# The FFN's input blocks turned by VectorE instead of TensorE in an attention-FFN kernel

## The chip, the cores and the metric

The kernel runs on one core of a Trainium2 chip. The metric is the device time of one execution in microseconds. The core has five engines that run their own instruction streams and wait for one another on semaphores: TensorE (PE; PEld is its weight load), VectorE (DVE), ScalarE (ACT), GpSimd (POOL) and SyncE (SP), whose work here is to issue transfers. Sixteen DMA engines carry the transfers of all queues.

## The reference

Four sequences of 2048 tokens of width 512, in float32. One attention layer, then a feed-forward layer (FFN), each followed by a LayerNorm:

```python
x = layernorm(x + attention(x) + x)          # causal, one head of width 512, its own LayerNorm with gamma, beta inside
probs = softmax(x @ wr.T)                    # router, 8 experts
routes, indices = top_k(probs, 2)
gates = routes / routes.sum(-1)
h = silu(x @ w1.T); h = silu(h @ w3.T); h = h @ w2.T
out = zeros_like(x)
for k in range(2): out = out.at[indices[:, k]].add(gates[:, k] * h)
x = layernorm(x + out)
```

Since `indices` are below 8, only the first eight rows of `out` get anything: sums over all 8192 tokens, weighted with their gates. The kernel therefore adds up the gated second hidden layer for each expert and multiplies the eight sums by `w2` at the very end. All other output rows are a LayerNorm of the attention's output.

## The kernel before

A float32 product is made of three passes with rounded operands (`split_product`, L330 to L335): high x high, high x low, low x high, on tiles of 128x128 weights and 128x512 data. Each operand is split by ScalarE, which writes the rounded high part, and VectorE, which subtracts it to get the low part.

**Attention** runs over four batches of 16 tiles of 128 query rows. It stores its normalised output x1 to a scratch tensor in DRAM, tile by tile, through SP's queue. In the last batch's tiles `load_w13` and `split_w13` bring in and split the FFN weights, which take the places of attention's weights (`m_hi` and `wvo_hi` in the rows stand for w1 and w3).

**The FFN** runs over 16 groups (`group(i, ...)` on each engine) of 512 tokens, one block of x1 of 512x512 each. A block is loaded to one half of `x1_in` with tokens on the partitions, two groups ahead (L401 to L405 on SP; the first two blocks by ScalarE's queue in its tile 14 of the last batch, L688 to L695). For the products it must have the features on the partitions. TensorE turns it in 16 transposes of 128x128 by the identity into PSUM banks 0 to 3 (`turn_x1`, L1279 to L1282); ScalarE rounds each bank to `x1t_hi` (L729 to L731), VectorE subtracts (`split_x1`, L1018 to L1020). For the next group's block eight transposes stand between the first and the second product, eight behind the second product's third tile, since they need banks that the products have left. The first block's 16 stand behind the last attention tile.

A group on TensorE: eight router matmuls (L1297 to L1299), the first product of 48 matmuls (with the last gate of the group before and four transposes of the router's logits behind its first quarter), eight transposes, the second product of 48 with two of the four gates (`gate`, L1284 to L1291) and eight transposes in it, and a third gate behind. The gates need the router's result. That comes by a chain: the logits are turned, VectorE subtracts the row maximum (`shifted`, L1039), POOL makes the exponential as a power (`expo`, L513), VectorE finds the two best and makes the gates (L1043 to L1069). In between VectorE subtracts for the first product's four Silu outputs (`split_h1`, L1026 to L1028) as ScalarE delivers them: the second and third behind `shifted`, the fourth behind the arg-max (L1054). The second product's chunk c waits for the c-th of them:

```python
for c in range(DC):
    if n == 0:
        pe.wait_ge(h1_ready, i * 4 + c + 1)
```

Each engine works through its instructions in the order in which they are written; nothing reorders them. Loops over batches and groups are hardware loops, with the last turn written out.

## Time and profile before

| | |
|---|---|
| time, median of 3 runs | 1711.9 us (1708.99 to 1712.27) |
| profiled execution, its own time | 1712.2 us |
| its span, first to last instruction | 1710.4 us |
| granted TensorE clock, mean | 0.997 |
| busy: PE, DVE, ACT, POOL | 98%, 46%, 39%, 17% of the span |
| FFN groups | the last 460 us of the span |

Rows of a timeline give the start in us from the span's start, the duration in us, the engine, the line of the kernel, the operation with what it writes and reads, and how often it stands in a row. In brackets is the time for which the engine was idle before, and what released it. A matmul's row runs to its modelled end, so rows of TensorE overlap; the distance of two starts tells what a step takes. The names are the program's without numbers: `x_in` is `x1_in`, `h_lo` is `h1_lo` or `h2_lo`.

### The profile page before, as it was taken

To read this page: it belongs to the slowest core of one execution; us is meant where nothing else is said; L and a number is where in the kernel's file an instruction comes from. 1 tells how busy PE (TensorE), PEld (TensorE's weight loads), DVE (VectorE), ACT (ScalarE), POOL (GpSimd) and SP (SyncE) were. 2 spreads that over 40 slices of the span, in tenths; PEclk is the share of its full clock that TensorE was granted. 3 is DMA by queue.
4 is the path that set the end of the run, shared out by engine and by line. 5 is a ranking of instruction groups with operands and counts; after the bars stand their busy time and mean duration, and the time that the engine had idled before them with its cause. 6 is when DMAs were issued, how large, how long until landed. Compare 5 with 4: busy or idle time off the path is not lost.

```text
span 1710.4 us, 23965 instructions
## 1 busy us (share of the span) xinstructions
PE 1680.0 (98%) x8179; PEld 1399.9 (82%) x8179; DVE 788.9 (46%) x2104; ACT 670.6 (39%) x1301; POOL 283.8 (17%) x491
## 2 busy tenths in 40 slices
PE   7999999999999999999999999999999999999998
PEld 5888888878888887888888888888878888888886
DVE  5454443455353455445334554534444444444443
ACT  4443433343342344344234443423344444444442
POOL 1120101121120111112011212201122121212111
PEclk9999999999999999999999999999999999999999
DMA  4111101121120112121111221112220101010100
GB/s 154 56 55 45 68 31 38 62 85 59 56 68 31 38 58 74 62 69 61 38 38 49 71 70 70 50 39 71 80 107 33 49 25 49 25 49 25 49 0 7
DMA packets 50116, 92.58 MB, mean 54 GB/s; under 512 B 5456, under 2 KB 5456, under 8 KB 50016
## 3 DMA queue, kind: packets, MB, share of 16 engines
q1 hardware_dynamic: 38064, 70.31, 11.7%
q10 hardware_dynamic: 11952, 20.99, 3.9%
q8 instruction: 57, 0.93, 0.2%
q14 instruction: 43, 0.35, 0.1%
HBM read 57.71 MB, written 33.57 MB: 53 GB/s over the span
## 4 chain that ended last, share of the span: by engine, by line
PE 80%; issue 12%; POOL 3%; ACT 3%; DVE 1%; DMA 0%; ACTq 0%; POOLq 0%; DVEq 0%
PE psum L333 24%; PE psum L335 24%; PE psum L334 23%; PE psum L1189 3%; PE psum L1281 2%; PE psum L1127 1%; POOL rstd L438 1%; ACT xin L564 1%; PE psum L1299 1%; PE psum L1298 1%; PE psum L1291 1%; PE psum L1290 1%; POOL expo L513 1%; ACT affine L548 1%; ACT tok L564 1%
## 5 line engine op out<-in xcount | busy, mean ns | idle before, releaser
L333 PE MATMUL psum<-xt_hi,g_hi 128*128 128x512 f32 (+3 forms) x640 | 240.2, 375 | 0.4 <-DVE g_lo L837 0.4
L335 PE MATMUL psum<-xt_lo,g_hi 128*128 128x512 f32 (+3 forms) x640 | 230.4, 360 | 0.0
L612 ACT ACTIVATE pt_hi<-psum 128x512 fp32r<-128x512 f32 (+3 forms) x160 | 84.9, 531 | 369.2 <-PE psum L1189 363.4
L334 PE MATMUL psum<-xt_hi,g_lo 128*128 128x512 f32 (+3 forms) x640 | 229.6, 359 | 0.0
L333 PE MATMUL psum<-v_hi,pt_hi 128*128 128x512 f32 x544 | 222.9, 410 | 1.6 <-DVE pt_lo L847 1.1
L335 PE MATMUL psum<-v_lo,pt_hi 128*128 128x512 f32 x544 | 213.1, 392 | 0.0
L334 PE MATMUL psum<-v_hi,pt_lo 128*128 128x512 f32 x544 | 212.8, 391 | 0.0
L435 POOL TENSOR_TENSOR var_eps<-meanvar,eps 128x2 f32<-128x2 f32 (+1 forms) x97 | 19.4, 200 | 1055.9 <-DVE meanvar L815 1051.5
L852 DVE TENSOR_REDUCE rowmax<-psum 128x1 f32<-128x512 f32 (+3 forms) x160 | 97.6, 610 | 198.3 <-PE psum L335 197.6
L734 ACT ACTIVATE act_f<-psum 128x512 f32<-128x512 f32 x128 | 76.6, 598 | 235.2 <-PE psum L335 235.2
L513 POOL TENSOR_TENSOR expo<-euler,shifted 128x32 f32<-128x32 f32 x16 | 87.3, 5457 | 319.5 <-DVE shifted L1039 319.5
L333 PEld LDWEIGHTS psum<-xt_hi,g_hi 128*128 128x128 f32 x640 | 121.6, 190 | 15.7 <-DVE g_lo L837 0.5
L335 PEld LDWEIGHTS psum<-xt_lo,g_hi 128*128 128x128 f32 x640 | 120.5, 188 | 16.1
L334 PEld LDWEIGHTS psum<-xt_hi,g_lo 128*128 128x128 f32 x640 | 121.2, 189 | 15.1
L847 DVE TENSOR_TENSOR pt_lo<-psum,pt_hi 128x512 fp32r<-128x512 f32 (+3 forms) x160 | 97.5, 609 | 77.2 <-ACT pt_hi L612 75.4
L335 PEld LDWEIGHTS psum<-v_lo,pt_hi 128*128 128x128 f32 x544 | 102.2, 188 | 23.0
L333 PEld LDWEIGHTS psum<-v_hi,pt_hi 128*128 128x128 f32 x544 | 102.3, 188 | 21.8 <-issue 2.9
L334 PEld LDWEIGHTS psum<-v_hi,pt_lo 128*128 128x128 f32 x544 | 102.6, 189 | 17.7
L564 ACT ACTIVATE tok<-tok,shift,rstd 128x512 f32<-128x512 f32 x128 | 97.3, 809 | 43.6 <-POOL shift L440 43.5
L596 ACT ACTIVATE probs<-psum,bias 128x512 f32<-128x512 f32 (+3 forms) x157 | 97.8, 628 | 25.9 <-PE psum L1189 11.6
L837 DVE TENSOR_TENSOR g_lo<-psum,g_hi 128x512 fp32r<-128x512 f32 x64 | 44.3, 692 | 131.0 <-ACT g_hi L561 131.0
L333 PE MATMUL psum<-wvo_hi,h_hi 128*128 128x512 f32 x256 | 102.5, 400 | 1.4 <-DVE h_lo L1028 1.4
(146 smaller groups left out, 3369.7 us busy)
## 6 DMA issues: line engine op xcount, KB each, us to landing
xin<-in_x ACTq DMA_DIRECT2D x64, 256.0 KB, 2.8
tok<-in_x SPq DMA_DIRECT2D x64, 256.0 KB, 2.6
x_scratch<-tok SPq DMA_DIRECT2D x64, 256.0 KB, 2.0
out_dram<-tok SPq DMA_DIRECT2D x64, 256.0 KB, 2.0
x_in<-x_scratch SPq DMA_DIRECT2D x14, 1024.0 KB, 5.6
xin<-in_w_t ACTq DMA_DIRECT2D x8, 256.0 KB, 2.8
x_in<-x_scratch ACTq DMA_DIRECT2D x2, 1024.0 KB, 8.0
w_sb<-in_w_t SPq DMA_DIRECT2D x1, 1024.0 KB, 5.6
```

Of the source, the lines that this page charges most:

```text
L333: pe.matmul(o, ws, ms, start=first, stop=False, skip_group_check=True)
L334: pe.matmul(o, w_lo, ms, start=False, stop=False, skip_group_check=True)
L335: return pe.matmul(o, ws, m_lo_, start=False, stop=last, skip_group_check=True)
L513: pool.tensor_tensor(expo[:], euler[:], shifted[:], ALU.pow).then_inc(exp_ready, 1)
L564: return act.activation(o, y, ACT.Identity, bias=shift[:, slot:slot + 1], scale=rstd[:, slot:slot + 1])
L596: act.activation(probs[:, at:at + w], psum[:, c, 0:w], ACT.Exp, bias=bias[:, t % 2:t % 2 + 1], scale=SCALE, accum_out=sums4[:, t % 2, c:c ...
L612: act.activation(pt_hi[:, n % 2, 0:w], psum[:, turn_bank(turn_use(t, c)), 0:w], ACT.Copy).then_inc(pt_hi_ready, 1)
L734: act.activation(act_f[:, n % 2, :], psum[:, bank, :], ACT.Silu)
L837: dve.tensor_tensor(g_lo[:, j, :], psum[:, j, :], g_hi[:, j, :], ALU.subtract).then_inc(g_ready, 1)
L847: dve.tensor_tensor(pt_lo[:, n % 2, 0:w], psum[:, turn_bank(turn_use(t, c)), 0:w], pt_hi[:, n % 2, 0:w], ALU.subtract).then_inc(pt_ready, 1)
L852: return dve.tensor_reduce((rowmax if chunks(t) == 1 else rowmax4)[:, c:c + 1], psum[:, c, 0:width(t, c)], AX.X, ALU.max)
L1189: last = pe.transpose(psum[:, turn_bank(n), k * P:(k + 1) * P], probs[:, key_start(t, c) + k * P:key_start(t, c) + (k + 1) * P], ident[:])
```

## The change

A block is loaded so that each 32x32 square lies in the quadrant of partitions to which it belongs when turned. The load is made of four transfers, one for each quadrant of 32 partitions, in pieces of 32 floats (128 B), 8192 to a block. VectorE then turns every 32x32 square in place with one 128x512 transpose for each 128 features (`dve.transpose`), four to a block, and writes a plain float32 tile `x1t_f`, from which ScalarE rounds and VectorE subtracts. TensorE's 256 transposes and their waits are gone. `h1_hi` and `h1_lo` move to other memory to make room for `x1t_f`. VectorE's group loop holds two groups, as its wait for the load goes by the half of `x1_in`.

```diff
-        x1_in = sb("x1_in", [P, 2, GROUP, D], F32, stage2)
+        x1_in = sb("x1_in", [P, 2, DC, GROUP * P], F32, stage2)
         x1t_hi = sb("x1t_hi", [P, DC, GROUP * P], F32R, stage2)
         x1t_lo = sb("x1t_lo", [P, DC, GROUP * P], F32R, stage2)
-        h1_hi = sb("h1_hi", [P, DC, GROUP * P], F32R, stage2)
-        h1_lo = sb("h1_lo", [P, DC, GROUP * P], F32R, stage2)
+        x1t_f = sb("x1t_f", [P, DC, GROUP * P], F32, stage2)
...
+        QUADRANTS, LANES = 4, 32
+        LOADS = QUADRANTS * DMA
+
+        def load_x1(engine, slot, first_row):
+
+            rows_of = x1_scratch[bass.ds(first_row, GROUP * P), :].rearrange("(t j) (c q i) -> q j c t i", j=LANES, q=QUADRANTS, i=LANES)
+            for q in range(QUADRANTS):
+                engine.dma_start(x1_in[q * LANES:(q + 1) * LANES, slot].rearrange("j c (t i) -> j c t i", i=LANES),
+                                 rows_of[q]).then_inc(x1_loaded[slot], DMA)
...
+            sp.wait_ge(scores_ready, B * CHUNKS)
+            for i in range(SLOTS):
+                sp.wait_ge(x1_stored[i], 2 * GROUP // SLOTS * DMA)
+            for i in range(2):
+                load_x1(sp, i, i * GROUP * P)
...
-                    sp.dma_start(x1_in[:, s], x1_scratch[bass.ds((2 * h + s) * 512, 512), :].rearrange("(t p) d -> p t d", p=P)).then_inc(x1_loaded[s], DMA)
+                    load_x1(sp, s, (2 * h + s) * (GROUP * P))
...
-                    for i in range(SLOTS):
-                        act.wait_ge(x1_stored[i], 2 * GROUP // SLOTS * DMA)
-                    for i in range(2):
-                        act.dma_start(x1_in[:, i], x1_scratch[i * 512:(i + 1) * 512, :].rearrange("(t p) d -> p t d", p=P)).then_inc(x1_loaded[i], DMA)
...
-                act.activation(x1t_hi[:, c, :], psum[:, c, :], ACT.Copy).then_inc(x1t_hi_ready, 1)
+                act.activation(x1t_hi[:, c, :], x1t_f[:, c, :], ACT.Copy).then_inc(x1t_hi_ready, 1)
...
+                if t == TILES - 1 and last:
+                    dve.wait_ge(x1_loaded[0], LOADS)
+                    turn_x1(0, 0)
+                    turn_x1(0, 1)
...
                 if chunks(t) > 2:
                     split_probs(b, t, 2)
+                if t == TILES - 1 and last:
+                    turn_x1(0, 2)
+                    turn_x1(0, 3)
...
+                    split_first_x1()
                     residual(b, TILES - 1)
-                    split_first_x1()
...
+            def turn_x1(slot, c):
+                dve.transpose(x1t_f[:, c, :], x1_in[:, slot, c, :]).then_inc(x1_turned, 1)
...
-                    dve.tensor_tensor(x1t_lo[:, c, :], psum[:, c, :], x1t_hi[:, c, :], ALU.subtract).then_inc(x1t_ready, 1)
+                    dve.tensor_tensor(x1t_lo[:, c, :], x1t_f[:, c, :], x1t_hi[:, c, :], ALU.subtract).then_inc(x1t_ready, 1)
...
+                if not last:
+                    dve.wait_ge(x1_loaded[1 - parity], loads)
+                    dve.wait_ge(x1t_ready, i * DC + DC)
+                    turn_x1(1 - parity, 0)
+                    turn_x1(1 - parity, 1)
                 split_h1(1)
+                if not last:
+                    turn_x1(1 - parity, 2)
+                    turn_x1(1 - parity, 3)
                 split_h1(2)
...
-            with dve.Fori(0, NG - 1) as i:
-                group(i, False)
+            with dve.Fori(0, NG // 2 - 1) as h:
+                group(2 * h, False, 0, h * LOADS + LOADS)
+                group(2 * h + 1, False, 1, h * LOADS + 2 * LOADS)
+            group(NG - 2, False, 0, NG // 2 * LOADS)
...
-            def turn_x1(slot, c):
-                for t in range(GROUP):
-                    last = pe.transpose(psum[:, c, t * P:(t + 1) * P], x1_in[:, slot, t, c * P:(c + 1) * P], ident[:])
-                last.then_inc(x1_turned, 1)
...
-                if not last_group:
-                    pe.wait_ge(x1_loaded[1 - parity], loads(parity))
-                    for c in range(2):
-                        pe.wait_ge(h1_hi_ready, 1 + i * 4 + c + 1)
-                        turn_x1(1 - parity, c)
...
-                    if n == 2 and not last_group:
-                        pe.wait_ge(x1t_ready, (i + 1) * DC + 2)
...
-                    if n == 2 and not last_group:
-                        for c in (2, 3):
-                            pe.wait_ge(h2_hi_ready, 1 + i * 4 + c - 1)
-                            turn_x1(1 - parity, c)
...
-            pe.wait_ge(x1_loaded[0], DMA)
             pe.wait_ge(probs_ready, 1 + B * CHUNKS)
-            for c in range(DC):
-                turn_x1(0, c)
```

**VectorE in a group**, from the shifted logits (`shifted`) to the sum of the exponentials (`esum`); `h_lo` is the subtraction for a Silu output. Before:

```order
L1039 TENSOR_TENSOR shifted<-logits,lmax 128x32 [waits rown]
L1027 REGISTER_ALU
L1028 TENSOR_TENSOR h_lo<-act_f,h_hi 128x512 [waits h1_hi_ready]
L1027 REGISTER_ALU
L1028 TENSOR_TENSOR h_lo<-act_f,h_hi 128x512 [waits h1_hi_ready]
L1043 TENSOR_REDUCE esum<-expo 128x4 [waits exp_ready]
```

After:

```order
L1061 TENSOR_TENSOR shifted<-logits,lmax 128x32 [waits rown]
L1063 ISA
L1064 REGISTER_ALU [waits x1_loaded1]
L994 STREAM_TRANSPOSE x1t_f<-x_in 128x512 [waits x1t_ready]
L994 STREAM_TRANSPOSE x1t_f<-x_in 128x512
L1049 REGISTER_ALU
L1050 TENSOR_TENSOR h_lo<-act_f,h_hi 128x512 [waits h1_hi_ready]
L994 STREAM_TRANSPOSE x1t_f<-x_in 128x512 x2
L1050 TENSOR_TENSOR h_lo<-act_f,h_hi 128x512 [waits h1_hi_ready]
L1073 TENSOR_REDUCE esum<-expo 128x4 [waits exp_ready]
```

Two transposes stand ahead of each of the two subtractions, the first behind a wait for the load.

**VectorE in the last attention tile and behind it**; `pt_lo` are the probabilities' third and fourth chunk, `wr_s` the router's weights, `tok` the last tile's residual. Before:

```order
L847 TENSOR_TENSOR pt_lo<-psum,pt_hi 128x512 [waits pt_hi_ready] x2
L970 CAST wr_s<-wr_raw 128x4x8 [waits wr_loaded,zeros_ready]
L972 TENSOR_TENSOR wr_s<-wr_raw,wr_s 128x4x8 [waits wr_hi]
L871 SCALAR_TENSOR_TENSOR tok<-psum,rinv,tok 128x512 [waits res_doubled,pv_done]
L977 TENSOR_TENSOR x1t_lo<-psum,x1t_hi 128x512 [waits x1t_hi_ready] x4
L811 BN_STATS stats<-tok 128x6 [waits attn_read,x1_ready,shift_ready]
```

After:

```order
L994 STREAM_TRANSPOSE x1t_f<-x_in 128x512 [waits x1_loaded0]
L994 STREAM_TRANSPOSE x1t_f<-x_in 128x512
L859 TENSOR_TENSOR pt_lo<-psum,pt_hi 128x512 [waits pt_hi_ready]
L994 STREAM_TRANSPOSE x1t_f<-x_in 128x512 x2
L859 TENSOR_TENSOR pt_lo<-psum,pt_hi 128x512 [waits pt_hi_ready]
L989 CAST wr_s<-wr_raw 128x4x8 [waits wr_loaded,zeros_ready]
L991 TENSOR_TENSOR wr_s<-wr_raw,wr_s 128x4x8 [waits wr_hi]
L999 TENSOR_TENSOR x1t_lo<-x1t_f,x1t_hi 128x512 [waits x1t_hi_ready] x4
L883 SCALAR_TENSOR_TENSOR tok<-psum,rinv,tok 128x512 [waits res_doubled,pv_done]
L823 BN_STATS stats<-tok 128x6 [waits attn_read,x1_ready,shift_ready]
```

Four transposes stand among the probabilities' chunks, and the subtractions for the first block have moved ahead of the residual.

**SP at the end of attention**; `x_scratch` are stores of x1, `out_dram` of the output, `w_sb` is w2. Before:

```order
L371 DMA tok<-in_x 128x512 [waits out_stored3]
L361 DMA x_scratch<-tok 128x512 [waits x1_ready]
L365 DMA out_dram<-tok 128x512 [waits out_ready]
L361 DMA x_scratch<-tok 128x512 [waits x1_ready] x2
L365 DMA out_dram<-tok 128x512 [waits out_ready] x2
L399 DMA w_sb<-in_w_t 128x4x512 [waits x1_stored3,x1_stored2,pv_done,x1_stored1,x1_stored0]
```

After:

```order
L372 DMA x_scratch<-tok 128x512 [waits x1_ready]
L376 DMA out_dram<-tok 128x512 [waits out_ready]
L345 DMA x_in<-x_scratch 32x64x32 [waits x1_stored2,x1_stored1,x1_stored3,x1_stored0,scores_ready]
L345 DMA x_in<-x_scratch 32x64x32 x7
L372 DMA x_scratch<-tok 128x512 [waits x1_ready] x2
L376 DMA out_dram<-tok 128x512 [waits out_ready] x2
L415 DMA w_sb<-in_w_t 128x4x512 [waits x1_stored3,x1_stored2,pv_done,x1_stored1,x1_stored0]
```

The eight transfers of the first two blocks stand on SP ahead of its last four stores; before, two transfers on ScalarE's queue did their work.

## Rows read from the trace of the kernel before

**Rows 1.** Page, first part: busy us (share of the span) and instructions
```profile
PE 1680.0 (98%) x8179; PEld 1399.9 (82%) x8179; DVE 788.9 (46%) x2104; ACT 670.6 (39%) x1301; POOL 283.8 (17%) x491
```

**Rows 2.** Timeline of POOL, groups 0, 2, 3: start us, us, engine, line, work
```profile
1262.95 5.82 POOL L513 TENSOR_TENSOR expo<-euler,shifted 128x32 f32<-128x32 f32 x1 [5.52 <-DVE shifted L1039]
...
1317.69 5.43 POOL L513 TENSOR_TENSOR expo<-euler,shifted 128x32 f32<-128x32 f32 x1 [22.23 <-DVE shifted L1039]
1345.36 5.43 POOL L513 TENSOR_TENSOR expo<-euler,shifted 128x32 f32<-128x32 f32 x1 [22.23 <-DVE shifted L1039]
```

**Rows 3.** Timeline of TensorE, group 1, eight transposes: start us, us, engine, line, work
```profile
1305.55 0.39 PE L335 MATMUL psum<-wvo_lo,h_hi 128*128 128x512 f32 x1
1305.79 1.03 PE L1281 MATMUL psum<-ident,x_in 128*128 128x128 f32 x8
...
1306.89 0.40 PE L334 MATMUL psum<-wvo_hi,h_lo 128*128 128x512 f32 x1
```

**Rows 4.** Timeline of TensorE, last group, second product
```profile
1683.61 0.39 PE L333 MATMUL psum<-wvo_hi,h_hi 128*128 128x512 f32 x1
...
1685.42 0.39 PE L335 MATMUL psum<-wvo_lo,h_hi 128*128 128x512 f32 x1
1685.74 0.50 PE L333 MATMUL psum<-wvo_hi,h_hi 128*128 128x512 f32 x1
1686.08 0.40 PE L334 MATMUL psum<-wvo_hi,h_lo 128*128 128x512 f32 x1
```

**Rows 5.** Timeline of VectorE, last group; in brackets idle us before, and releaser
```profile
1684.99 0.69 DVE L1028 TENSOR_TENSOR h_lo<-act_f,h_hi 128x512 fp32r<-128x512 f32 x1 [0.43 <-ACT h_hi L735]
```

**Rows 6.** The timeline of TensorE at the change of stage and in group 0
```profile
1245.06 0.49 PE L333 MATMUL psum<-v_hi,pt_hi 128*128 128x512 f32 x1
...
1250.65 1.91 PE L1281 MATMUL psum<-ident,x_in 128*128 128x128 f32 x16
...
1255.02 0.39 PE L333 MATMUL psum<-x1t_hi,m_hi 128*128 128x512 f32 x1
...
1271.38 0.50 PE L333 MATMUL psum<-wvo_hi,h_hi 128*128 128x512 f32 x1 [1.44 <-DVE h_lo L1028]
```

**Rows 7.** The timeline of VectorE in the last attention tile and behind it
```profile
1242.77 0.69 DVE L847 TENSOR_TENSOR pt_lo<-psum,pt_hi 128x512 fp32r<-128x512 f32 x1 [1.79 <-ACT pt_hi L612]
1245.98 0.69 DVE L847 TENSOR_TENSOR pt_lo<-psum,pt_hi 128x512 fp32r<-128x512 f32 x1 [2.52 <-ACT pt_hi L612]
...
1251.92 1.29 DVE L977 TENSOR_TENSOR x1t_lo<-psum,x1t_hi 128x512 fp32r<-128x512 f32 x2 [0.32 <-ACT x1t_hi L731]
```

**Rows 8.** The timeline of POOL at the change of stage
```profile
1251.67 0.29 POOL L502 TENSOR_SCALAR_AFFINE_SELECT fold_rows<-fold_rows 128x128 f32<-128x128 f32 x1
```

**Rows 9.** The timeline of VectorE: groups 0 (first row) and 2
```profile
1262.79 0.69 DVE L1028 TENSOR_TENSOR h_lo<-act_f,h_hi 128x512 fp32r<-128x512 f32 x1
...
1319.82 0.69 DVE L1028 TENSOR_TENSOR h_lo<-act_f,h_hi 128x512 fp32r<-128x512 f32 x1 [2.21 <-ACT h_hi L735]
1322.54 0.69 DVE L1028 TENSOR_TENSOR h_lo<-act_f,h_hi 128x512 fp32r<-128x512 f32 x1 [2.03 <-ACT h_hi L735]
1323.16 0.19 DVE L1043 TENSOR_REDUCE esum<-expo 128x4 f32<-128x32 f32 x1
```

**Rows 10.** The page's third part: SP's queue
```profile
q1 hardware_dynamic: 38064, 70.31, 11.7%
```

**Rows 11.** Timelines of SP's and ScalarE's queues, transfers at the change of stage
```profile
1234.55 0.58 SPq L365 DMA_DIRECT2D out_dram<-tok  x1
...
1232.55 0.53 ACTq L694 DMA_DIRECT2D x_in<-x_scratch  x1
...
1233.11 0.53 ACTq L695 DMA_DIRECT2D wr_raw<-in_wr_t  x1
```

**Rows 12.** Tiles of the block, then of the router weight: their loads
```profile
DMA to landing us min/median/max: 5.5/5.6/10.2
...
DMA to landing us min/median/max: 10.2/10.2/10.2
```

More of the change, by code:

```diff
@@ L239, in attention_mlp @@
         wr_raw = sb("wr_raw", [P, DC, E], F32, stage2)
-        taken = 2 * GROUP * D + 4 * DC * GROUP * P + DC * P + GROUP * P + 4 * D + DC * E
+        taken = 2 * GROUP * D + 3 * DC * GROUP * P + DC * P + GROUP * P + 4 * D + DC * E
         sb("not_yet_free", [P, 2 * DC * S - taken + (1 + SLOTS) * D], F32, stage2)
+        h1_hi = sb("h1_hi", [P, DC, GROUP * P], F32R, stage2)
+        h1_lo = sb("h1_lo", [P, DC, GROUP * P], F32R, stage2)
         act_f = sb("act_f", [P, 2, D], F32, stage2)
@@ L1005, in _, with group @@
             ROUTE = 15
-            def group(i, last):
+            def group(i, last, parity, loads):
                 count = [0]
@@ L1077, in group @@
                     split_h2(n)
-            with dve.Fori(0, NG - 1) as i:
-                group(i, False)
+            with dve.Fori(0, NG // 2 - 1) as h:
+                group(2 * h, False, 0, h * LOADS + LOADS)
+                group(2 * h + 1, False, 1, h * LOADS + 2 * LOADS)
+            group(NG - 2, False, 0, NG // 2 * LOADS)
             at_batch[0], count[0] = B - 1, last_own[0]
             norm_behind(B, 0, 1, 2)
-            group(NG - 1, True)
+            group(NG - 1, True, 1, 0)
             dve.wait_ge(rows_loaded, DMA)
@@ L1291, in gate, with group @@
                 pe.matmul(psum[:, ACC, :], gates_s[:, n, :], h2_lo[:, n % 2, :], start=False, stop=False, skip_group_check=True).then_inc(gated, 1)
-            def group(i, last_group, parity):
+            def group(i):
                 pe.wait_ge(logits_copied, 1 + i)
@@ L1351, in _ @@
                 for parity in range(2):
-                    def loads(parity_):
-                        return h * DMA + (1 + parity_) * DMA
-                    group(2 * h + parity, False, parity)
-            def loads(parity_):
-                return (NG // 2) * DMA
-            group(NG - 2, False, 0)
-            group(NG - 1, True, 1)
+                    group(2 * h + parity)
+            group(NG - 2)
+            group(NG - 1)
             gate(NG - 1, 3)
```

14 lines of the change are left out of this document (7 added, 7 removed).

## The prediction

> **What bounds the kernel now.** I read the page's first part, then the timelines of the FFN groups engine by engine, then the change of stage. TensorE is busy 98% of the span [rows 1], so work counts if it is taken from TensorE's own row or ends a wait of it. The exponentials of two successive groups start 27.67 us apart, and fifteen of the sixteen groups hold sixteen transposes in two runs of eight [rows 2, 3].
>
> A run of eight costs more than its place. From the start of the matmul before it to the start of the second one after it are 1306.89 - 1305.55 = 1.34 us [rows 3]. An ordinary step is (1685.42 - 1683.61) / 8 = 0.226 us [rows 4], so two steps would take 0.45 us, and a run costs **0.89 us**.
>
> What stands right behind the bound is told by the last group, which has no transposes and so has already what the change makes of all others. There the fourth chunk of the second product waits for VectorE: from 1685.42 to 1686.08 are 0.66 us in place of 0.45, **0.21 us** lost [rows 4]. VectorE was itself idle 0.43 us before that subtraction, waiting for ScalarE [rows 5]. So the router chain (shifted logits, POOL's exponential of 5.43 us, the arg-max, then the fourth subtraction) can come 0.43 us later before it costs anything, and all beyond that is TensorE's.
>
> **The change part by part.**
> *Removed from TensorE in the loop.* Groups 1 to 14 lose two runs each and get the last group's stall: 14 x (2 x 0.89 - 0.21) = 22.0 us. Group 0 loses its second run, 0.9 us. Its first run lies ahead of a stall of 1.44 us on the fourth subtraction [rows 6] and is counted with the change of stage.
>
> *The change of stage.* Now TensorE turns the first block from 1250.65 and starts the first product at 1255.02 [rows 6], while VectorE makes four subtractions (0.32 us idle, 2.48 us busy) ahead of the last tile's LayerNorm statistics [rows 7]. After the change the four turnings, roundings and subtractions are due before the last attention matmul ends. TensorE is then held by the router's fold matrix, ready at 1251.67 + 0.29 = 1251.96 [rows 8], and eight logit matmuls of 0.226 bring the first product to about 1253.8, 1.2 us earlier. The statistics, and with them ScalarE's first Silu, the first exponential and the subtraction behind which TensorE stalls, come 2.48 + 0.32 less some overlap, **2.7 us** earlier. TensorE comes 1.2 + 0.9 = 2.1 us earlier to a place where it waits 1.44 us now; so it still waits there, and what is won up to it is the chain's 2.7 us.
>
> *Added to VectorE.* Four 128x512 transposes a group. No such instruction is in the trace. From below: it writes as much as a 128x512 subtraction, and no row here of that size is under 0.6 us a piece (2.48 us for four [rows 7]). From above I take twice, 1.4 us. I take 0.69, the row of the same shape and type, about 0.65 where two follow each other. Two stand ahead of the second subtraction of the group, where VectorE idles 2.21 us, two ahead of the third, where it idles 2.03 us [rows 9]: 1.3 us fits in each, cost nothing. If that cover went, the chain of 0.43 us slack would pay. At 1.4 us each the second subtraction is 0.6 late, the third 0.6 + 2.8 - 2.03 = 1.4, and 1.4 - 0.43, some 1 us, is lost a group. The subtraction for the block itself and the rounding on ScalarE keep count and shape and only read SBUF instead of PSUM; the group's other subtractions read SBUF already, at 0.69 us [rows 9]. I give them nothing. TensorE's wait ahead of the second product's third tile goes, too; I give nothing for it.
>
> *Added waits.* VectorE waits for the load before it turns. Behind that wait stand, in the groups, the second subtraction and the whole router chain; in the last attention tile, the subtraction of the probabilities that TensorE's third chunk needs.
>
> *The loads.* One megabyte comes as 8192 pieces of 128 B, in place of 512 of 2 KB: 512 on each of 16 DMA engines. SP's queue took 38064 packets of 1.85 KB in 11.7% of 16 engines, 84 ns each [rows 10]. By bytes a piece is 84 x 128 / 1847 = 5.8 ns, 3.0 us for the megabyte, and nothing excludes a little less; if a piece costs as much as a whole packet, 43 us. The nearest row is the router weight's load, 512 pieces of 32 B. It was queued behind two block loads, of which the second landed by 1232.55 + 10.2 = 1242.75 and it at 1233.11 + 10.2 = 1243.31 [rows 11, 12]: 0.56 us for 32 pieces an engine, 17 ns each, **9 us** for the megabyte. I take that, since it is a row of small pieces. In the groups it costs nothing: a load is issued two groups ahead and 9 us is well under the 26.1 us in which a group will want one (27.67 - 1.78 + 0.21). SP waits on nothing new there.
>
> At the change of stage it costs. The two first loads move from ScalarE's queue to SP's, behind the store at 1234.55 that takes 0.58 us to issue [rows 11]; so from 1235.1. A 2 KB load landed after 5.5 us at best [rows 12], 2.7 of them its 32 packets an engine, so 2.8 are fixed: the first block is there at 1235.1 + 2.8 + 9 = 1246.9. TensorE takes up the third chunk at 1245.06 [rows 6]; two transposes (1.3) and the subtraction (0.69) have to come before, so it had to land by 1243.1. **3.8 us** lost. With 3 us a megabyte it lands at 1240.9, and the transposes fall into idle times of 1.79 and 2.52 us [rows 7], at no cost; with 43 it is 38 us. SP's last stores come behind these loads in the queue; with 9 us each the loads are done before the stores matter.
>
> *The sum.* 22.0 + 0.9 + 2.7 - 3.8 = 21.8 us. Against the profiled execution's 1712.2 us that is **1690.4 us**; the median of the runs shown is 0.3 lower, so 1690.
>
> **The rivals.**
> *A, the router chain comes late: 1702 us.* The transposes start with POOL's exponential. The first group's exponential took 5.82 us and not 5.43; it began 0.16 us into a VectorE subtraction of 0.69 us with both operands in SBUF [rows 2, 9]. If two transposes hold it off in that way, the chain is 1.2 us late, less 0.43 of slack 0.8 us, in 15 groups 12 us. Transposes of 1.4 us would cost about as much. Against it: in all later groups the same subtraction starts inside the exponential and lengthens nothing, and a transpose reads one tensor, not two. The Trainium skill (SBUF — State Buffer, Who interferes with whom) says that a VectorE instruction with two SBUF inputs, or in a two-port mode, locks out a GpSimd instruction that reads SBUF, and one with a single input outside those modes does not. The first group's 5.82 us agrees with its first half; by the other half the sum stays 1690, unless the transpose runs in a two-port mode, when it is 1702, and no run here shows that yet.
>
> *B, the loads bound the groups: slower.* From 27.67 us / 512 = 54 ns a piece on, each group waits for its load and the kernel is slower. At 84 ns sixteen loads of 43 us from 1235.1 end at 1926; in the old trace the last but one group's exponential, which the last load would now precede, stands at 1317.69 + 12 x 27.67 = 1649.7, 60.7 before the end of the span at 1710.4: about 1987 us. For it: small pieces, and nothing in the trace at 128 B. Against it: 17 ns at 32 B, a third of the threshold. The Trainium skill (DMA: Bandwidth & Descriptors, Rules for kernel authors) advises against a transposition by a plain DMA with a rearranged pattern, which it puts at 19 times the hardware transpose. Taken as 19 times the 2.7 us in which the packets moved, an estimate of 51 us a megabyte, the sum would be beyond 2100 us; the pieces here stay contiguous for 128 B, and no run here shows such a load.
>
> *C, only the first load is late: 1693 to 1706 us.* Pieces of 23 to 50 ns hide in the groups but land the first block at 1250 to 1264, a stall of 7 to 20 us once.
>
> **How the numbers follow.** The forecast has 0.57 (1684 to 1693: no stall at the first load gives 1686.6, one of 6 us 1692.6, and 2 us below are for my other terms), A 0.20, C 0.13, B 0.08, and 0.02 that gains and stalls cancel. The range 1684 to 1704 holds the forecast, A and most of C, some 8 in 10. About 0.2%, 3.4 us, is what a measurement of this kernel can tell from no change. Faster by more: 0.88; within: 0.03; slower: 0.09, B with a little of C.
>
> **What would show it.** Right: no transposes of the block on TensorE; exponentials 26.1 us apart and still 5.43 us; VectorE transposes of about 0.69 us; one TensorE stall of some 4 us at the third chunk of the last attention tile, ended by VectorE behind a DMA. Wrong: exponentials over 6 us or a larger stall at the fourth subtraction (A), block loads landing 26 us or more after their issue (B), or a stall over 7 us at that chunk (C).

## The result, and the profile after

The changed kernel takes **1683.3 us** (median of 4 runs, 1681.75 to 1684.82) against 1710.57 (4 runs, 1708.99 to 1712.27): a ratio of 0.9841, 95% interval 0.9829 to 0.9853. Its profiled execution took 1682.32 us, its span is 1680.3. The forecast was 1690 in 1684 to 1704: the direction and the mechanism held, but the gain is larger than forecast, and the time falls 0.7 us under the range. Two executions, one of the kernel before (6010 us) and one with 64 B pieces (4291 us), stand far outside all others and are left out of the comparisons.

The page after, parts 1 and 3, against [rows 1, 10]: TensorE has 256 matmuls fewer (the transposes of sixteen groups) and 29.6 us less busy time, VectorE 39 us more, and SP's queue 124,700 packets more.

```profile
PE 1650.4 (98%) x7923; PEld 1369.7 (82%) x7923; DVE 828.1 (49%) x2168; ACT 671.6 (40%) x1301; POOL 282.6 (17%) x491
...
q1 hardware_dynamic: 162768, 72.41, 15.8%
```

POOL's timeline, groups 0, 2 and 3, against [rows 2]: the exponentials follow each other after 26.09 us in place of 27.67, and each takes 5.43, that of group 0 too.

```profile
1258.04 5.43 POOL L529 TENSOR_TENSOR expo<-euler,shifted 128x32 f32<-128x32 f32 x1 [5.53 <-DVE shifted L1061]
...
1309.90 5.43 POOL L529 TENSOR_TENSOR expo<-euler,shifted 128x32 f32<-128x32 f32 x1 [20.65 <-DVE shifted L1061]
1335.99 5.43 POOL L529 TENSOR_TENSOR expo<-euler,shifted 128x32 f32<-128x32 f32 x1 [20.66 <-DVE shifted L1061]
```

VectorE's timeline in group 3, against [rows 9] (in brackets the idle us before, and what ended it): each pair of transposes takes 1.31 us and lies where VectorE was idle. Of 2.21 us of idle time ahead of the second subtraction 0.93 are left, of 2.03 ahead of the third 0.81, and ahead of the fourth 0.38.

```profile
1335.89 1.31 DVE L994 STREAM_TRANSPOSE x1t_f<-x_in 128x512 f32<-128x512 f32 x2
1338.12 0.69 DVE L1050 TENSOR_TENSOR h_lo<-act_f,h_hi 128x512 fp32r<-128x512 f32 x1 [0.93 <-ACT h_hi L747]
1338.73 1.30 DVE L994 STREAM_TRANSPOSE x1t_f<-x_in 128x512 f32<-128x512 f32 x2
1340.84 0.69 DVE L1050 TENSOR_TENSOR h_lo<-act_f,h_hi 128x512 fp32r<-128x512 f32 x1 [0.81 <-ACT h_hi L747]
1341.46 0.18 DVE L1073 TENSOR_REDUCE esum<-expo 128x4 f32<-128x32 f32 x1
...
1343.56 0.69 DVE L1050 TENSOR_TENSOR h_lo<-act_f,h_hi 128x512 fp32r<-128x512 f32 x1 [0.38 <-ACT h_hi L747]
```

TensorE's timeline at the change of stage, against [rows 6]: the second chunk of the last attention tile, the third, the zeroing behind attention, the first logit matmul, the first product, and the first group's fourth chunk. The forecast stall of 3.8 us at the third chunk is 0.30.

```profile
1235.79 0.47 PE L334 MATMUL psum<-v_hi,pt_hi 128*128 128x512 f32 x1 [1.07 <-DVE pt_lo L859]
...
1242.73 0.50 PE L334 MATMUL psum<-v_hi,pt_hi 128*128 128x512 f32 x1 [0.30 <-DVE pt_lo L859]
...
1248.32 0.39 PE L1359 MATMUL psum<-h_hi,gates_s 128*128 128x512 f32 x1
1249.96 0.49 PE L1325 MATMUL psum<-x1t_hi,wr_s 128*128 128x512 f32 x1 [1.25 <-POOL fold_rows L518]
...
1251.90 0.39 PE L334 MATMUL psum<-x1t_hi,m_hi 128*128 128x512 f32 x1
...
1266.10 0.50 PE L334 MATMUL psum<-wvo_hi,h_hi 128*128 128x512 f32 x1 [0.18 <-DVE h_lo L1050]
```

**Where the time went.** The first of these rows is a landmark: the change touches nothing ahead of it, and the same matmul with the same 1.07 us of idle time stands in every trace. In the kernel before it is the first row here; the second is the last group's exponential, and the fence behind it has the same exponential of the kernel after:

```profile
1238.65 0.47 PE L333 MATMUL psum<-v_hi,pt_hi 128*128 128x512 f32 x1 [1.07 <-DVE pt_lo L847]
...
1677.36 5.45 POOL L513 TENSOR_TENSOR expo<-euler,shifted 128x32 f32<-128x32 f32 x1 [3.70 <-DVE shifted L1039]
```

```profile
1648.95 5.45 POOL L529 TENSOR_TENSOR expo<-euler,shifted 128x32 f32<-128x32 f32 x1 [3.70 <-DVE shifted L1061]
```

Distances from it, before and after (us): to the end of attention, 12.00 and 12.53 (**0.53 lost**, the stall and the first matmul behind it); from there to the first group's fourth chunk, 20.73 and 17.78 (**2.95 won**); from there to the last group's exponential (1677.36 and 1648.95), 405.98 and 382.85 (**23.13 won**); from there to the end of the span, 33.0 and 31.35 (1.7 won). The landmark itself comes 2.86 us earlier. So of the 30.1 us between the two spans 25.55 are the change's, and 4.55 lie where it changes nothing. Most of this is TensorE's clock. The windows of the kernel before (the window, its length, the busy us of PE, PEld, DVE, ACT and POOL, then the granted clock, the DMA share and GB/s) show that it fell from 2.4 GHz, its upper level, in part of three of them, each time after an idle stretch of TensorE (2.51 us at 26, 2.13 at 371, 1.45 and 0.73 in the tail).

```profile
20.00:30.00 10.00, 7.49 (x30) 5.79 (x29) 7.63 (x16) 5.81 (x11) 2.38 (x4) 0.85 0.00 0
...
370.00:380.00 10.00, 8.49 (x37) 6.70 (x37) 4.96 (x13) 3.03 (x5) 2.28 (x5) 0.83 0.33 110
...
1695.00:1703.00 8.00, 5.82 (x19) 3.55 (x18) 0.69 (x1) 2.79 (x7) 0.00 (x0) 0.79 0.00 0
```

The kernel after shows 1.00 in all three places. Matmul against matmul the kernel before is 0.5 us behind it at 26 us, where TensorE waited for ScalarE's first blocks, 1.4 at 31 us and 2.7 at 380: of the 2.86 us ahead of the landmark some 2.2 lie in the two windows with a fall of the clock, and 0.5 ahead of them. In the tail, the last eight matmuls of the kernel after take 3.62 us, those of the kernel before 4.72:

```profile
1671.74 3.62 PE L1379 MATMUL psum<-w_sb,acc_t 128*128 128x512 f32 x8
```

```profile
1700.70 4.72 PE L1372 MATMUL psum<-w_sb,acc_t 128*128 128x512 f32 x8
```

### The profile page after: what moved, and what is told of

It reads as the page before. It is cut to its first block, busy times and chain, and to the rows that moved or that the text cites. A ratio compares the mean times of both kernels' runs of the same rounds, so it can differ in the third digit from the quotient of the medians.

```text
span 1680.3 us, 23574 instructions
## 1 busy us (share of the span) xinstructions
PE 1650.4 (98%) x7923; PEld 1369.7 (82%) x7923; DVE 828.1 (49%) x2168; ACT 671.6 (40%) x1301; POOL 282.6 (17%) x491
## 3 DMA queue, kind: packets, MB, share of 16 engines
q1 hardware_dynamic: 162768, 72.41, 15.8%
## 4 chain that ended last, share of the span: by engine, by line
PE 79%; issue 13%; POOL 3%; ACT 3%; DVE 2%; DMA 1%; SPq 0%; ACTq 0%; POOLq 0%; DVEq 0%
PE psum L334 24%; PE psum L336 24%; PE psum L335 24%; PE psum L1221 3%; PE psum L1159 1%; POOL rstd L454 1%; PE psum L1326 1%; PE psum L1325 1%; PE psum L1318 1%; PE psum L1317 1%; ACT xin L580 1%; ACT tok L580 1%; POOL expo L529 1%; ACT affine L564 0%; DVE stats L823 0%
## 5 line engine op out<-in xcount | busy, mean ns | idle before, releaser
L853 DVE TENSOR_TENSOR v_lo<-psum,v_hi 128x512 fp32r<-128x512 f32 x64 | 44.0, 688 | 121.4 <-ACT v_hi L602 121.4
```

## The experiments

A time is a median of runs beside runs of the kernel before on the same chip; the ratio is to those. Because falls of the clock and the first loads move a run by 4 us and more, the last column compares traces, one for each kernel, from the landmark to the end of the span, less what the tail's transposes and last matmuls took over the 4.62 us that they take at the full clock. Two traces of the same kernel agree in it to 0.3 us.

| kernel | median us | ratio, 95% interval | landmark to end |
|---|---|---|---|
| before | 1710.57 | | 470.1 |
| before, again | 1711.27 | 1.0007 [0.9998, 1.0016] | 470.1 |
| after | 1683.3 | 0.9841 [0.9829, 0.9853] | 444.5 |
| after, again | 1684.64 | 0.9852 [0.9834, 0.9869] | 444.2 |
| subtractions put back | 1687.57 | 0.9869 [0.9854, 0.9884] | 446.1 |
| TensorE transposes put back | 1707.44 | 0.9983 [0.9974, 0.9992] | 467.8 |
| VectorE transposes twice | 1686.96 | 0.9865 [0.9850, 0.9880] | 446.2 |
| copies for transposes | 1684.6 | 0.9855 [0.9834, 0.9875] | 445.4 |
| 2 KB pieces | 1684.82 | 0.9852 [0.9833, 0.9870] | 444.0 |
| 64 B pieces | 1689.9 | 0.9875 [0.9856, 0.9893] | 452.1 |
| 32 B pieces | 1715.97 | 1.0035 [1.0020, 1.0050] | 474.4 |
| eight issues a block | 1691.42 | 0.9889 [0.9872, 0.9905] | 451.5 |
| late low half | 1681.49 | 0.9830 [0.9816, 0.9844] | 441.6 |
| late low half, change of stage | 1681.03 | 0.9824 [0.9810, 0.9838] | 439.5 |

### Both kernels again, beside the clock

No edit. Of the kernel before:

> The kernel before, unchanged, to see TensorE's granted clock beside each time. Theory (the change's own steps are worth about 25 us; the rest of the 27.3 measured is that runs of the kernel before lose more to falls of TensorE's clock): runs at a mean clock of 1.000 take about 1707.5 us (1712.2 less 1.7 in the tail, less 2.9 before the change of stage), runs at 0.998 to 0.999 about 1709 to 1710, runs at 0.997 about 1712. Rival (a term of the change is under-sized by 2 us): runs at 1.000 take 1709 or more.

Its eleven runs took 1708.39 (mean clock 0.999) to 1713.27 (0.997); of the 20 runs of the kernel before beside them one stood at 1.000, with 1708.45. The new trace has its landmark here, 3.8 us earlier than the first, and the same distance to the end:

```profile
1234.84 0.47 PE L333 MATMUL psum<-v_hi,pt_hi 128*128 128x512 f32 x1 [1.07 <-DVE pt_lo L847]
```

So a run's time goes with its clock and its start as expected, though the expected 1707.5 at 1.000 was 1 us too low. Of the kernel after:

> The changed kernel, unchanged, for more of its times beside the mean granted clock. Theory (the change is worth 25.5 us at equal clock; the measured 27.3 hold some 2 us by which few runs differ in falls of TensorE's clock and in the first loads): the difference of the medians over many runs comes out between 25 and 26.5 us; runs at a mean clock of 1.000 stand 24.5 to 26 us below the runs of the kernel before at 1.000 or 0.999. Rival (the change also spares falls of the clock in the tail): the difference stays at 27 us or more, and most of its runs stand at 1.000.

It took 1681.8, 1683.68, 1685.59 and 1685.87 us at 1.000, 0.999, 0.998 and 0.997. Here the difference of the medians is 1710.44 - 1684.64 = 25.8, between 25 and 26.5, and from the landmark it is 470.1 - 444.2 = 25.9. At 0.999 on both sides it is 24.1 to 25.9; the run at 1.000 stands 26.0 to 27.8 under those at 0.999, more than expected, but none of the kernel before stood at 1.000 beside it. The change is worth some 25.6 us; the 27.3 of the first comparison hold 1 to 2 us by which few executions differ, in falls of the clock and in the first loads. Whether the kernel after loses a little less to falls of the clock than the one before, too few of its runs tell.

### TensorE's transposes put back

```diff
+            def turn_const(c):
+                for t in range(GROUP):
+                    pe.transpose(psum[:, c, t * P:(t + 1) * P], fold_rows[:], ident[:])
...
+                    for c in range(2):
+                        pe.wait_ge(h1_hi_ready, 1 + i * 4 + c + 1)
+                        turn_const(c)
...
+                        for c in (2, 3):
+                            pe.wait_ge(h2_hi_ready, 1 + i * 4 + c - 1)
+                            turn_const(c)
```

> The changed kernel with two runs of eight TensorE transposes a group put back where they were, of a constant matrix and with nobody waiting for them. Theory (the loop's gain is those runs, 2 x 0.89 less the 0.13 to 0.2 of stall that they cover): exponentials 27.65 us apart, 15 groups x 1.58 = 23.7 us slower than the changed kernel, about 1706. Rival (a good part of the gain came from the waits that went, for the load and for the subtractions ahead of the third tile): under 18 us slower, and exponentials under 27.3 apart.

From the landmark 467.8 - 444.5 = 23.3 us more, by the medians 22.8 to 24.1; the exponentials, of which these are the first and the last, are 27.63 apart:

```profile
1259.85 5.43 POOL L529 TENSOR_TENSOR expo<-euler,shifted 128x32 f32<-128x32 f32 x1 [5.54 <-DVE shifted L1061]
...
1674.30 5.44 POOL L529 TENSOR_TENSOR expo<-euler,shifted 128x32 f32<-128x32 f32 x1 [3.70 <-DVE shifted L1061]
```

The loop's gain is TensorE's own row and nothing else: the waits stay out here, and the exponentials are as far apart as in the kernel before (from 1262.95 to 1677.36, 27.63), so the vanished waits give nothing. The remaining 470.1 - 467.8 = 2.3 us to the kernel before are the change of stage.

### The subtractions put back behind the residual

```diff
-                    split_first_x1()
                     residual(b, TILES - 1)
+                    split_first_x1()
```

> The changed kernel with the first block's four subtractions put back behind the last residual. Theory (in front of the residual they start the LayerNorm statistics, and with them the chain to the first group's fourth subtraction, 2.5 us earlier): 2.3 to 2.7 us slower than the changed kernel, about 1685.8, with TensorE idle 1.5 to 2.7 us at that fourth subtraction in place of 0.18. Rival (the chain earlier comes from the transposes taken off TensorE, and the place of the subtractions decides nothing): under 0.5 us.

In the kernel before, the four subtractions took 2.48 us ahead of the statistics:

```profile
1251.92 2.48 DVE L977 TENSOR_TENSOR x1t_lo<-psum,x1t_hi 128x512 fp32r<-128x512 f32 x4 [0.32 <-ACT x1t_hi L731]
```

TensorE's timeline with them put back, zeroing and fourth chunk:

```profile
1251.04 0.39 PE L1359 MATMUL psum<-h_hi,gates_s 128*128 128x512 f32 x1
...
1271.10 0.50 PE L334 MATMUL psum<-wvo_hi,h_hi 128*128 128x512 f32 x1 [1.96 <-DVE h_lo L1050]
```

These are 20.06 us in place of 17.78, **2.3 us** more, with 1.96 idle in place of 0.18. Of the 2.95 us won at the change of stage 2.3 come from the place of the subtractions alone. From the landmark it is 1.6, since in this run the first block was in time and the third chunk did not stall.

### VectorE's transposes twice

```diff
+                if twice:
+                    dve.transpose(spare[:, c, :], x1_in[:, slot, c, :])
                 dve.transpose(x1t_f[:, c, :], x1_in[:, slot, c, :]).then_inc(x1_turned, 1)
```

> The changed kernel with every transpose of VectorE in the loop made twice (the first time into a spare tile), 5.2 us a group in place of 2.6. Theory (cover of 0.93 us idle ahead of the second subtraction, 0.81 ahead of the third, 0.38 ahead of the fourth): the second is 0.37 late, the third 0.37 + 1.3 - 0.81 = 0.86, the fourth 0.86 - 0.38 = 0.48, which TensorE pays: 15 x 0.48 = 7 us slower than the changed kernel, about 1690, exponentials still 5.43 us. Rival A of the prediction (transposes hold the exponential off): exponentials of 6 us and more and over 15 us slower. A third way (the chain has more slack than these idle times): under 2 us.

A miss: 446.2 - 444.5 = **1.7 us**, not 7, and exponentials 26.18 apart, 0.1 more. VectorE's timeline of group 3:

```profile
1336.92 0.71 DVE L996 STREAM_TRANSPOSE spare<-x_in 128x512 f32<-128x512 f32 x1
...
1339.34 0.65 DVE L1053 TENSOR_TENSOR h_lo<-act_f,h_hi 128x512 fp32r<-128x512 f32 x1
...
1342.31 0.65 DVE L1053 TENSOR_TENSOR h_lo<-act_f,h_hi 128x512 fp32r<-128x512 f32 x1
```

Four transposes in a row take 2.42 us, 0.60 each, where I had put 0.65 a piece on top of the pairs' 1.3; a subtraction behind them starts the next 0.57 later. So the third subtraction is some 0.4 late and not 0.86, and the 0.38 ahead of the fourth take nearly all of it. The cover is what the idle times say; the length of the row was wrong. (The 1.7 us are 1.9 if the third chunk's stall is counted, which is 0.05 us in this trace; the loop alone gives 15 x 0.12.) The exponentials stay at 5.43 us beside four transposes, so rival A's mechanism is out for this instruction.

### Copies in place of the transposes

```diff
-                dve.transpose(x1t_f[:, c, :], x1_in[:, slot, c, :]).then_inc(x1_turned, 1)
+                dve.tensor_copy(x1t_f[:, c, :], x1_in[:, slot, c, :]).then_inc(x1_turned, 1)
```

> The changed kernel with each transpose of VectorE replaced by a copy of the same 128x512 between the same two tiles; the turning within 32x32 squares is left out. Theory (rival A fell because the transpose, with one input, doesn't lock GpSimd out; a copy, which may run in a two-port mode, does): the copy takes under 0.5 us, and the exponentials, which start 0.1 us into the first copy, take 0.2 to 0.9 us more than 5.43. The second and third subtractions of the group don't get later, and the chain's slack of 0.4 us takes most of it: 0 to 4 us slower than the changed kernel. Rival (nothing of this shape holds the exponential off): 5.43 us, and the same time within 1 us.

POOL's and VectorE's timelines, group 3:

```profile
1338.34 5.61 POOL L529 TENSOR_TENSOR expo<-euler,shifted 128x32 f32<-128x32 f32 x1 [20.41 <-DVE shifted L1061]
...
1338.24 0.82 DVE L994 COPY x1t_f<-x_in 128x512 f32<-128x512 f32 x2
...
1341.08 0.76 DVE L994 COPY x1t_f<-x_in 128x512 f32<-128x512 f32 x2
```

A copy takes 0.41 us, and the exponential started 0.1 into one takes 5.61 to 5.64 in the first fourteen groups; the chain's slack absorbs it. The Trainium skill (SBUF — State Buffer, Who interferes with whom) names copies, casts and tensor-scalar operations as those that can enter a two-port mode and then contend with GpSimd, and excepts an instruction with one SBUF input outside those modes. The 0.2 us beside copies agree, and so do the 5.43 us beside a transpose, which has one input. Rival A's mechanism exists, then, but for the copy, and at 0.2 us an exponential. An exponential under way doesn't hold a copy off: the third and fourth stand inside it and take 0.76 us together. POOL's zeroing does: at the change of stage the first copy waits behind that of two tiles, and the pair takes 2.17 us in place of 0.8.

```profile
1241.64 0.96 POOL L510 MEMSET h_hi<- 128x1024 f32 x1
1242.54 0.95 POOL L510 MEMSET h_lo<- 128x1024 f32 x1
...
1241.94 2.17 DVE L994 COPY x1t_f<-x_in 128x512 f32<-128x512 f32 x2 [2.64 <-DMA x_in<-x_scratch]
```

In the kernel after the transposes run beside the same two instructions in 1.31 us a pair. The copies' wait makes TensorE idle 1.16 us at the third chunk in place of 0.30; that is the 0.9 us by which this kernel is slower in the table, and the loop is as fast.

### Larger and smaller pieces

Whole rows of 2 KB, without the exchange of quadrants:

```diff
-                engine.dma_start(x1_in[q * LANES:(q + 1) * LANES, slot].rearrange("j c (t i) -> j c t i", i=LANES),
-                                 rows_of[q]).then_inc(x1_loaded[slot], DMA)
+                first = first_row + q * P
+                engine.dma_start(x1_in[:, slot, q, :], x1_scratch[bass.ds(first, P), :]).then_inc(x1_loaded[slot], DMA)
```

> The changed kernel with each load of a quadrant replaced by a load of 128 whole rows, pieces of 2 KB; VectorE's transposes stay, and the exchange of quadrants is left out. Theory (small pieces cost nothing but the first block's lateness): the first block lands 3 to 5 us earlier, VectorE waits nothing for it, TensorE has no idle time at the third chunk, and the time is 0.3 to 0.6 us under that of the changed kernel, which is as good as no change. Rival (many small packets also cost elsewhere, in the last stores or in VectorE's or POOL's work): over 2 us faster.

444.0 in place of 444.5, and no wait for the load: all that 128 B pieces cost this kernel is half a microsecond, once. It is often less: of six more traces with the loads of the kernel after, TensorE idles 0 to 0.05 us at the third chunk in five and 0.31 in one. Then pieces of 64 B and of 32 B, by two or four loads a quadrant, each with the same 2048 pieces (the edit for 64 B; for 32 B the step is 8):

```diff
+                for a in range(0, LANES, 16):
+                    engine.dma_start(to[:, :, :, a:a + 16], rows_of[q][:, :, :, a:a + 16]).then_inc(x1_loaded[slot], DMA)
```

> The changed kernel with each quadrant's load cut into four loads of 32 B pieces, 32768 pieces a block in place of 8192. Theory (the price of a piece, not of a byte, sets a load's time, about 13 ns for 128 B and 9 to 13 for 32 B): 2048 pieces an engine are 18 to 27 us a block; the first block comes 12 to 20 us late, once, in the last attention tile, and in the groups a load stays under or just at the 26.1 us that it has: 1694 to 1705 us. Rival (the issues or the pieces bind the groups, over 26.1 us a block): exponentials over 27 us apart and over 1715 us. The prediction's 17 ns would be 35 us a block, and over 1800.

> The changed kernel with each quadrant's load cut into two loads of 64 B pieces, 16384 pieces a block. Theory (a load lands 3.2 us and 10.5 ns for each of an engine's pieces after its first issue, by the two points at hand, 8.6 us at 512 pieces and 24.8 at 2048): the first block lands 14 us after the first issue, 5.4 later than in the changed kernel; TensorE idles 5 to 6 us at the third chunk, and the time is 5 to 8 us above the changed kernel's, 1689 to 1692, with exponentials 26.08 apart. Rival (the number of issues sets it, eight a block at some 1.2 us): 11 us or less, and a stall under 3 us; or (bytes set it) 8.6 us and no more stall than now.

The first block lands 8.6 us after SP's first issue with 128 B (1232.20 to 1240.79), 13.8 with 64 B, 24.8 with 32 B. TensorE idles 0.30, 5.48 and 16.54 us at the third chunk, and in the loop the exponentials stay 26.05 to 26.09 apart. First the kernel after: its loads in the view of the block's tile, SP's queue (8 issues take 11.44 us, 1.43 each) and VectorE; then TensorE with 64 B pieces; then with 32 B pieces SP, VectorE, TensorE and ScalarE:

```profile
DMA to landing us min/median/max: 3.3/4.2/5.9
```

```profile
1232.20 11.44 SPq L345 DMA_DIRECT2D x_in<-x_scratch  x8
...
1240.79 1.31 DVE L994 STREAM_TRANSPOSE x1t_f<-x_in 128x512 f32<-128x512 f32 x2 [2.69 <-DMA x_in<-x_scratch]
```

```profile
1249.90 0.79 PE L334 MATMUL psum<-v_hi,pt_hi 128*128 128x512 f32 x1 [5.48 <-DVE pt_lo L860]
```

```profile
1233.36 29.64 SPq L347 DMA_DIRECT2D x_in<-x_scratch  x21
...
1258.18 1.30 DVE L995 STREAM_TRANSPOSE x1t_f<-x_in 128x512 f32<-128x512 f32 x2 [18.92 <-DMA x_in<-x_scratch]
...
1260.12 0.79 PE L334 MATMUL psum<-v_hi,pt_hi 128*128 128x512 f32 x1 [16.54 <-DVE pt_lo L860]
...
1282.93 0.81 ACT L581 ACTIVATE tok<-tok,shift,rstd 128x512 f32<-128x512 f32 x1 [9.81 <-DMA x_scratch<-tok]
...
1288.15 0.79 PE L334 MATMUL psum<-wvo_hi,h_hi 128*128 128x512 f32 x1 [4.49 <-ACT h_hi L748]
```

The 64 B run comes out as expected. With 32 B two more things go wrong, which I had not expected: the last store of a tile stands behind the loads on SP's queue, ScalarE waits 9.81 us for it and TensorE 4.49 for ScalarE, and the matmul behind the long stall takes 0.79 us in place of 0.50, at the lower clock. So 1716, and not 1694 to 1705. The loop isn't bound even at a quarter of the piece.

### Eight issues a block, pieces as in the change

In the two experiments above pieces and issues grow together. Here the pieces stay, and each load of a quadrant is made in two of 16 partitions:

```diff
+                for a in (0, 16):
+                    engine.dma_start(x1_in[q * LANES + a:q * LANES + a + 16, slot].rearrange("j c (t i) -> j c t i", i=LANES),
+                                     rows_of[q][a:a + 16]).then_inc(x1_loaded[slot], DMA)
```

> The changed kernel with each quadrant's load cut into two loads of 16 partitions: eight issues a block as with 64 B pieces, but 8192 pieces of 128 B as in the changed kernel. Theory (the number of pieces sets when a block lands): an issue takes SP half as long, about 0.7 us in place of 1.43 where eight follow each other, the first block lands 8 to 9.5 us after the first issue, TensorE idles under 1 us at the third chunk, and the time is that of the changed kernel within 1 us. Rival (the number of issues sets it, 1.43 us each): 14 us, TensorE idles 5 to 6 us there, and the time is 5 to 8 us above.

SP's queue, its first three issues and all sixteen, then TensorE and the queue's share:

```profile
1233.01 2.15 SPq L346 DMA_DIRECT2D x_in<-x_scratch  x3
```

```profile
1233.01 19.31 SPq L346 DMA_DIRECT2D x_in<-x_scratch  x16
...
1248.30 0.79 PE L334 MATMUL psum<-v_hi,pt_hi 128*128 128x512 f32 x1 [5.06 <-DVE pt_lo L860]
...
q1 hardware_dynamic: 163792, 72.41, 24.5%
```

My theory falls: the block lands after 13.4 us, and TensorE idles 5.06, about what the rival says. Over the four kernels the number of loads orders the landings (4, 8, 8 and 16 loads a block: 8.6, 13.8, 13.4 and 24.8 us), and the number of pieces doesn't (8192, 16384, 8192 and 32768). But that SP's issuing sets them isn't shown: the first three issues take 0.72 us each, as my theory has it, and all sixteen 1.21 on average, so something that no row shows holds up the later ones. And a third thing changed, the number of partitions a load covers. With 2 KB pieces q1 holds 12.5% of 16 engines over 1682.8 us, with 128 B pieces 15.8% over 1680.3, so 131072 pieces take 881 us more than the 8192 packets of 84 ns [rows 10] that they replace: 12 ns a piece. By the same sum a piece takes 30 ns of an engine when a load covers 16 partitions and not 32. What sets the landing, SP's issues or the pieces in the engines, **stays open**; these runs give only the price of whole loads.

### A faster version

The gap that is left in every group is at the fourth chunk. TensorE may do the two matmuls that need only the high half first (`ready` waits for the fourth subtraction):

```diff
+            pe.matmul(o, ws, ms, start=first, stop=False, skip_group_check=True)
+            pe.matmul(o, ws, m_lo_, start=False, stop=False, skip_group_check=True)
+            ready()
+            return pe.matmul(o, w_lo, ms, start=False, stop=last, skip_group_check=True)
```

> The changed kernel; in the fourth chunk of the second product's first tile TensorE makes the two matmuls of the high half first and waits for the low half (the fourth subtraction) only ahead of the third. Theory (what is left of the stall behind the fourth subtraction is 0.13 to 0.2 us in each of sixteen groups and is the low half's lateness alone): exponentials 25.9 to 25.95 us apart in place of 26.08, 2 to 3 us faster than the changed kernel, about 1682 against its 1684 over eight runs. Rival (the gap belongs to the switch of operands, or ScalarE's high half is as late): 26.05 or more, and the same time within 1 us.

The exponentials stand 25.91 us apart, 0.17 less, and the distance from the landmark is 2.9 us less, as expected:

```profile
1336.06 5.43 POOL L537 TENSOR_TENSOR expo<-euler,shifted 128x32 f32<-128x32 f32 x1 [20.48 <-DVE shifted L1069]
1361.97 5.43 POOL L537 TENSOR_TENSOR expo<-euler,shifted 128x32 f32<-128x32 f32 x1 [20.48 <-DVE shifted L1069]
```

And the change of stage, where `fold_rows` gets a place that is free before attention ends, POOL builds it ahead of its wait for that end, and ScalarE's group 0 is taken out of its loop:

```diff
         wr_raw = sb("wr_raw", [P, DC, E], F32, stage2)
+        fold_rows = sb("fold_rows", [P, P], F32, stage2)
...
-            pool.wait_ge(pv_done, 1 + B * CHUNKS)
             pool.memset(fold_rows[:], 0.0).then_inc(fold_memset, 1)
...
+                    if first and n == 1:
+                        norm_behind(B - 1, TILES - 1)
...
-            norm_behind(B - 1, TILES - 1)
-            with act.Fori(0, NG - 1) as i:
+            group(0, False, True)
+            with act.Fori(1, NG - 1) as i:
```

> As the run before, and the change of stage: the router's fold matrix is built ahead of the attention's end, in a tile of its own, and ScalarE makes the first group's first Silu ahead of the last tile's two normalisations. Theory (the first product then starts with the zeroing, 1.2 us earlier, and the first exponential follows it, not the LayerNorm): the first exponential some 1.5 to 2 us earlier after the end of attention (9.72 us now), and 1.2 to 2 us off the time beyond the run before, 3.5 to 5 us under the changed kernel, about 1680. Rival (TensorE only waits more at the first group's fourth subtraction): under 0.5 us beyond the run before.

The first exponential comes 1259.08 - 1251.46 = 7.62 us after the end of attention in place of 9.72, and from the landmark another 2.1 us are gone, 0.4 of them because the third chunk didn't wait in this trace:

```profile
1251.46 0.39 PE L1374 MATMUL psum<-h_hi,gates_s 128*128 128x512 f32 x1
...
1259.08 5.44 POOL L537 TENSOR_TENSOR expo<-euler,shifted 128x32 f32<-128x32 f32 x1 [3.43 <-DVE shifted L1071]
```

The medians, 1681.49 and 1681.03, don't separate the two versions: no run of the second stood at a clock of 1.000. They are faster than the kernel before by 1.7 and 1.8%, and their medians lie below both of the changed kernel's, though single runs overlap with its runs (1679.57 to 1683.33 against 1681.75 to 1685.87); beyond the late low half the gain is shown in one trace only.

## Why the prediction was right or wrong

- **TensorE's transposes, 22.0 + 0.9: right.** 23.1 measured in the traces, 23.3 when they are put back. A run of eight costs 0.89 us, and what is left behind it is the last group's small stall, as it was read from [rows 4].
- **VectorE's transposes, nothing: right.** 0.668 to 0.714 us each, 1.31 a pair, in idle times that keep 0.93 and 0.81. Even made twice they cost under 2 us.
- **Change of stage, 2.7: right.** 2.95; 2.3 of it are the place of the four subtractions, which the experiment took back alone. One step inside was off: the first product starts 3.58 us after attention's end (1251.90 - 1248.32) in place of 4.37 (1255.02 - 1250.65), so 0.8 us earlier and not 1.2. TensorE therefore waits only 0.18 us at the fourth chunk, but the chain still ends last there, as forecast, and the term stands.
- **The first load, 3.8: wrong, and this is the step that failed.** It took 17 ns for a piece from the router weight's landing behind two block loads [rows 11, 12], so 9 us for a block and a landing 11.8 us after the first issue. The block landed after 8.6, by the same fixed 2.8 some 11 ns a piece, and TensorE lost 0.53 in place of 3.8 (in other traces less). The mechanism, one stall at the third chunk ended by VectorE behind a DMA, was right, and it grows as described when the pieces are made smaller; the term was 3.3 us too large. The size of the pieces isn't what misled: with pieces of the router weight's 32 B a block, 2048 pieces an engine, landed after 24.8 us, by the same sum again 11 ns each. What else the 0.56 us between the two landings held no row shows, and whether the pieces or SP's issues set the 8.6 us stays open. The lower bound's 5.8 ns would have given no stall, which is nearer to what happened.
- **The time that the sum was taken from, 1712.2: wrong too, and it is why the time came out under the range.** With the load's 0.5 in place of 3.8 the sum is 1687.1, still inside. But 1712.2 us was a run with falls of the clock both ahead of the landmark and in the tail, 1.6 us over the median of its four runs, and the range had nothing for that. Against the profiled run terms and base account for the miss: 1690.4 less 3.3 (load), 0.5 (the other terms), 1.7 (tail) and 2.9 (ahead of the landmark, 2.2 of it clock) is 1682.0, and the profiled run took 1682.3. The last 0.7 us are within the spread of the executions (1681.75 to 1684.82): over all eight runs of the kernel after the median is 1684.0, the end of the range.
- **Rivals.** A didn't happen, as exponentials of 5.43 us show; even the copy, which does lengthen them, does so by 0.2 us, inside the slack of 0.43, and A's 12 us are shown for no instruction. B didn't happen: a load of 256 KB lands 3.3 to 5.9 us after its issue, and even 32 B pieces leave the period alone, so the warning of the Trainium skill (DMA: Bandwidth & Descriptors, Rules for kernel authors), 19 times for a transposition by plain DMA, doesn't bear on an exchange that keeps 128 B together: the prediction's estimate from it was 51 us a block, and the block landed after 8.6; the 54 ns at which the loop would be bound were not reached. C happened to the extent of half a microsecond at most; with 64 and 32 B pieces the stall that it describes came.

## What to carry to other kernels

Work that sits on the bounding engine's own row can be costed to a few per cent from a place in the same trace that lacks it (here the last group), and work moved into another engine's idle time is free as long as each idle stretch, taken one by one, holds it. The price of a new kind of transfer deserves bounds and a place where its lateness can hurt: here the first one only, since all later ones have two groups of lead. Before a forecast of 1% is made from one profile, find out what that execution itself lost; a landmark ahead of the change, the same row in every trace, separates that from what the change does.

## What the hardware showed that I had not expected

- TensorE's clock fell from 2.4 GHz to its lower level for short stretches after idle stretches of TensorE of 0.7 to 2.5 us, in some executions and not in others with about the same idle time: windows of 0.79, 0.83 and 0.85 before, 1.00 after. In the tail it costs 1.6 us.
- A VectorE transpose of 128x512 takes 0.67 to 0.71 us by its row, but in a row one starts every 0.60.
- A copy of 128x512 takes 0.41 us and lengthens an exponential of POOL by 0.2 us, and POOL's zeroing of 128x1024 holds it off (a pair takes 2.17 us in place of 0.8); neither happens with a transpose.
- SP's issue of a load takes 0.49 us with 128 pieces of 2 KB (8 in 3.90 us) and 1.43 with 2048 pieces of 128 B; by the queue's share a piece of 128 B takes about 12 ns of an engine, and 30 when the load covers 16 partitions instead of 32.
